# A twelve-block decoder on one core: GpSimd order, early first scores and a vector-engine causal mask in the last stage

## The reference, cut to what matters

```python
# stage 3x: linear cross attention, 16 heads of 16; f(x) = x + 1 if x > 0 else exp(x)
q = f(query @ Wq.T); gate = sigmoid(query @ Wg.T + bg); k, v = split(kv @ Wkv.T); k = f(k)
z = 1 / (q . k.sum(-2) + EPS)
out = (q @ (k^T v) * z) * gate @ Wo.T

# stage 3f: B_, S, D = 8, 128, 256; F_ = 1024; R = 16; H = 16; HD = 16
x = _rmsnorm(hidden_states, ln1_w)
scores = einsum('bqhd,bkhd->bhqk', q, k) / sqrt(HD)
scores = where(causal, scores, finfo.min)
attn = einsum('bhqk,bkhd->bqhd', softmax(scores), v) @ Wo.T
mod = 0.1 * tanh(attn @ A)
h = _rmsnorm(residual, ln2_w)
gate = silu(h @ W_in_base.T + mod * (h @ A) @ B)
up = h @ W_up_base.T
return residual + gate * up @ W_down.T
...
x = x + _L3_xattn_ref(_layernorm(x), ctx, ...)
x = x + _L3_ffn_ref(_layernorm(x), ...)
```

## Time and profile before

| | us |
|---|---|
| median of 3 runs | 2128.72 |
| lowest, highest of the 3 | 2124.98, 2131.11 |
| the profiled execution | 2125.13 |
| its span, first to last instruction | 2123.4 |

### The profile page before, as it was taken

How to read it: one execution, slowest core, us unless ns; L and a number is a source line. 1 busy time by engine, 2 the same in 40 slices (tenths; PEclk the granted TensorE clock), 3 DMA queues, 4 the chain that set the end, 5 groups by cost and what they waited for, 6 DMA issues and landing times.

```text
span 2123.4 us, 31457 instructions
## 1 busy us (share of the span) xinstructions
PE 1850.7 (87%) x11530; PEld 1378.9 (65%) x11530; DVE 1470.8 (69%) x2483; ACT 1073.9 (51%) x2328; POOL 1088.7 (51%) x797
## 2 busy tenths in 40 slices
PE   7577779789899987899999999868888789998999
PEld 6111148545689965677777777757777565566887
DVE  5698952456764476777777776589999978855453
ACT  4444421334322254666666666566666656654443
POOL 2599950211692065655555554599999840022321
PEclk9688989689899999999999999989999999999999
DMA  4211001130400000110000001000000020000000
GB/s 161 48 35 35 0 1 40 38 159 0 179 1 1 1 21 21 50 34 1 1 2 1 1 1 40 20 1 1 1 1 1 25 76 7 1 1 1 6 9 8
DMA packets 22177, 54.88 MB, mean 26 GB/s; under 512 B 8591, under 2 KB 13752, under 8 KB 19592
## 3 DMA queue, kind: packets, MB, share of 16 engines
q1 hardware_dynamic: 22024, 52.88, 7.4%
HBM read 44.48 MB, written 1.05 MB: 21 GB/s over the span
## 4 chain that ended last, share of the span: by engine, by line
PE 54%; DVE 18%; POOL 11%; issue 9%; ACT 7%; SPq 1%; DMA 0%; DVEq 0%; POOLq 0%; ACTq 0%
POOL sbuf L1310 4%; PE psum L4136 4%; DVE sbuf L2302 4%; PE psum L4199 3%; PE psum L3490 2%; DVE psum L3113 2%; POOL sbuf L1318 2%; PE psum L4296 2%; PE psum L4583 1%; PE psum L4604 1%; PE psum L4590 1%; PE psum L4168 1%; PE psum L4184 1%; PE psum L4140 1%; PE psum L4148 1%
## 5 line engine op out<-in xcount | busy, mean ns | idle before, releaser
L1310 POOL TENSOR_TENSOR sbuf<-sbuf 128x1035 f32<-128x1035 f32 x128 | 248.2, 1967 | 0.9 <-ACT sbuf L1952 0.9
L4296 PE MATMUL psum<-sbuf 128*128 128x128 f32 (+1 forms) x1024 | 144.8, 292 | 60.9 <-ACT sbuf L1979 45.4
L1979 ACT ACTIVATE sbuf<-sbuf 128x1001 f32<-128x1001 f32 (+1 forms) x128 | 141.8, 1138 | 101.1 <-DVE sbuf L3121 69.0
L4296 PEld LDWEIGHTS psum<-sbuf 128*128 128x128 f32 (+1 forms) x1024 | 126.3, 153 | 82.3 <-ACT sbuf L1979 63.9
L1265 POOL TENSOR_TENSOR sbuf<-sbuf 128x512 f32<-128x512 f32 x64 | 66.7, 1042 | 184.8 <-DVE sbuf L2985 184.8
L1111 POOL TENSOR_TENSOR sbuf<-sbuf 128x1024 f32<-128x1024 f32 x64 | 149.9, 2355 | 15.9 <-DVE sbuf L2302 15.1
L2302 DVE TENSOR_TENSOR_SCAN sbuf<-psum,sbuf 128x1024 f32<-128x1024 f32 x64 | 144.6, 2277 | 13.7 <-ACT psum L1439 7.0
L3438 PE MATMUL psum<-sbuf 96*128 96x512 bf16 x256 | 84.2, 440 | 74.9 <-DVE sbuf L2302 32.3
L1893 ACT ACTIVATE sbuf<-psum,sbuf 128x128 f32<-128x128 f32 x256 | 90.4, 365 | 107.2 <-DVE sbuf L2979 107.2
L1439 ACT ACTIVATE psum<-psum,sbuf 128x1016 f32<-128x1016 f32 x64 | 68.9, 1081 | 125.3 <-PE psum L3438 125.3
L3113 DVE SCALAR_TENSOR_TENSOR psum<-sbuf,psum 128x1024 f32<-128x1024 f32 (+1 forms) x96 | 122.2, 1273 | 12.3 <-PE psum L4286 5.3
(11 more groups left out here) (809 smaller groups left out, 5105.3 us busy)
## 6 DMA issues: line engine op xcount, KB each, us to landing
sbuf<-sbuf SPq DMA_DIRECT2D x42, 128.0 KB, 2.4
sbuf<-w_p_d SPq DMA_DIRECT2D x8, 512.0 KB, 3.8
sbuf<-w_qkv_d SPq DMA_DIRECT2D x3, 768.0 KB, 4.2
sbuf<-w_e_d SPq DMA_DIRECT2D x1, 2048.0 KB, 7.8
sbuf<-w_gu_d SPq DMA_DIRECT2D x1, 2048.0 KB, 9.0
sbuf<-w_gu_d SPq DMA_DIRECT2D x2, 1024.0 KB, 7.7
sbuf<-w_dn_d SPq DMA_DIRECT2D x1, 2048.0 KB, 15.8
sbuf<-w_q_d SPq DMA_DIRECT2D x1, 2048.0 KB, 8.0
```

What stands on the lines that cost most here:

```text
L1310: pool.tensor_tensor(P_r[g % 7][:, :, :], rows.unsqueeze(2).to_broadcast([128, 23, 45]), cols.unsqueeze(1).to_broadcast([128, 23, 45]), AL ...
L1979: act.activation(Q_r[g % 6][:, 0:w], Q_r[g % 6][:, 0:w], ACT.Silu, scale=q8_p[n % 2][:, h:h + 1]).then_inc(silu_done, 1)
L4296: last = pe.matmul(Gps[0:m, c, :], Q_r[g % 6][:, 128 * c:128 * c + m], ident[:, :], start=h == 0 and c % 4 == 0, stop=h == 7, skip_group_c ...
```

## The change

The diff does the following.

- POOL, stage 3x: in each turn `L3x_unit(i + 3)` is called ahead of `L3x_softplus(i + 1)`.
- The first element's steps of stage 3f move up. On PE: transposes from turn 6 to 5, q and k from 7 to 6, value and scores from behind the loop to turn 8 ahead of `L3x_project(7)`; the product `L3f_woap` goes ahead of `L3x_project(6)`. On ACT: `L3f_unT(0)` and `L3f_qTc(0)` go to the top of turns 6 and 7. On DVE: `L3f_keys(0)` goes into turn 7.
- The mask: the four matmuls of each `L3f_scores` go. `L3f_max` first adds the mask (f32, broadcast over the 8 heads) to the scores in PSUM and writes `L3f_P` in SBUF, waits for that, and takes the maximum from SBUF; `L3f_sub` works in place on `L3f_P`. The wait for the transposes of the element before moves from `L3f_sub` to `L3f_max`.
- The order in a pass of stage 3f: on ACT `L3f_qTc(i + 1)` behind both `L3f_exp`; on DVE `L3f_keys(i + 1)` behind both `L3f_sums`; on PE `L3f_ups(i - 1, 1)` ahead of `L3f_value(i + 1)`.

```diff
@@ POOL, stage 3x
             for i in range(-1, 8):
+                if i < 5:
+                    L3x_unit(i + 3)
                 if i < 7:
                     L3x_softplus(i + 1)
-                if i < 5:
-                    L3x_unit(i + 3)
                 if i >= 0:
                     L3x_logs(i)
@@ ACT, stage 3x and 3f
             for i in range(9):
+                if i == 6:
+                    L3f_unT(0)
+                if i == 7:
+                    L3f_qTc(0)
                 if i < 6:
                     L3x_kexp(i + 2)
...
-                if i == 6:
-                    L3f_unT(0)
                 if i == 7:
                     act.wait_ge(woa_done, 1)
                     act.activation(L3f_woa[:, :, :], L3f_woap[:, :, :], ACT.Copy).then_inc(woac_done, 1)
-                    L3f_qTc(0)
...
-                if i < 7:
-                    L3f_qTc(i + 1)
                 if i < 8:
                     L3f_exp(i, 0)
                     L3f_exp(i, 1)
                 if i < 7:
+                    L3f_qTc(i + 1)
                     L3f_vc(i + 1)
@@ DVE
             def L3f_max(n, a):
                 dve.wait_ge(score_done, L3f_start['score'] + n + 1)
                 if n > 0:
-                    dve.wait_ge(sub_done, L3f_start['sub'] + 2 * n + a - 1)
-                dve.tensor_reduce(L3f_mx[a][:, :], L3f_S8[a][:, :, :], AX.X, ALU.max).then_inc(max_done, 1)
+                    dve.wait_ge(pT_done, L3f_start['pT'] + 2 * n + a - 1)
+                dve.tensor_tensor(L3f_P[a][:, :, :], L3f_S8[a][:, :, :], causal[:, None, :].to_broadcast([128, 8, 128]), ALU.add).then_inc(mask_done, 1)
+                dve.wait_ge(mask_done, L3f_start['mask'] + 2 * n + a + 1)
+                dve.tensor_reduce(L3f_mx[a][:, :], L3f_P[a][:, :, :], AX.X, ALU.max).then_inc(max_done, 1)
             def L3f_sub(n, a):
                 dve.wait_ge(max_done, L3f_start['max'] + 2 * n + a + 1)
-                if n > 0:
-                    dve.wait_ge(pT_done, L3f_start['pT'] + 2 * n + a - 1)
-                dve.tensor_tensor(L3f_P[a][:, :, :], L3f_S8[a][:, :, :], L3f_mx[a][:, :].unsqueeze(2).to_broadcast([128, 8, 128]), ALU.subtract).then_inc(sub_done, 1)
+                dve.tensor_tensor(L3f_P[a][:, :, :], L3f_P[a][:, :, :], L3f_mx[a][:, :].unsqueeze(2).to_broadcast([128, 8, 128]), ALU.subtract).then_inc(sub_done, 1)
...
+                if i == 7:
+                    dve.wait_ge(const_done, L3f_start['const'] + 1)
+                    L3f_keys(0)
                 if i < 8:
                     L3x_quotient(i)
                 if i > 0:
                     L3x_resid(i - 1)
-            dve.wait_ge(const_done, L3f_start['const'] + 1)
-            L3f_keys(0)
             L3f_hidden(1)
...
-                if i < 7:
-                    L3f_keys(i + 1)
                 if i < 8:
                     L3f_sums(i, 0)
                     L3f_sums(i, 1)
+                if i < 7:
+                    L3f_keys(i + 1)
@@ PE
-                for r in range(4):
-                    pe.matmul(L3f_S[:, r, :, :, :], idb[:, :], L3f_causal[:, None, :].to_broadcast([128, 4, 128]), start=True, stop=False)
                 for c in range(2):
                     for r in range(4):
-                        last = pe.matmul(L3f_S[:, r, c, :, :], L3f_qT[32 * r:32 * r + 32, c, :], L3f_kM[32 * r:32 * r + 32, c, :, :], start=False, stop=c == 1)
+                        last = pe.matmul(L3f_S[:, r, c, :, :], L3f_qT[32 * r:32 * r + 32, c, :], L3f_kM[32 * r:32 * r + 32, c, :, :], start=True, stop=True)
...
                 if i < 8:
                     L3x_readout(i)
-                if i > 0:
-                    L3x_project(i - 1)
-                if i == 6:
-                    pe.wait_ge(L3f_w_loaded, 144)
-                    pe.wait_ge(L3x_unT_done, 8)
-                    L3f_uTr(0)
                 if i == 7:
...
                     last.then_inc(woa_done, 1)
+                if i == 8:
+                    L3f_value(0)
+                    pe.wait_ge(woac_done, 1)
+                    L3f_scores(0)
+                if i > 0:
+                    L3x_project(i - 1)
+                if i == 5:
+                    pe.wait_ge(L3x_unT_done, 8)
+                    L3f_uTr(0)
+                if i == 6:
+                    pe.wait_ge(L3f_w_loaded, 144)
                     L3f_qk(0)
-            L3f_value(0)
-            pe.wait_ge(woac_done, 1)
             for i in range(9):
-                if i < 8:
+                if 0 < i < 8:
                     L3f_scores(i)
...
                 if i > 0:
                     L3f_gates(i - 1, 1)
+                if i > 0:
+                    L3f_ups(i - 1, 1)
                 if i < 7:
                     L3f_value(i + 1)
                 if i > 0:
-                    L3f_ups(i - 1, 1)
                     L3f_adapt(i - 1, 1)
                     L3f_downs(i - 1, 0)
```

More of the change, by code:

```diff
@@ L707, in build_program @@
         L3f_start = {'const': 10, 'bn': 54, 'stats': 70, 'u': 46, 'uT': 34, 'unT': 34, 'q': 81, 'v': 84, 'ss': 68, 'lnvar': 85, 'rstd': 85, 'vc': 92,
-                     'qTc': 81, 'kTc': 84, 'score': 116, 'max': 128, 'exp': 136, 'recip': 92, 'prob': 68, 'pT': 120, 'pTc': 120, 'o': 92, 'cat': 79,
-                     'proj': 108, 'resid': 60, 'sub': 64, 'ur': 8, 'xr': 16, 'mod': 4, 'low': 4, 't': 4, 'gate': 20, 'up': 20, 'silu': 144,
-                     'prod': 136}
+                     'qTc': 81, 'kTc': 84, 'score': 116, 'mask': 129, 'max': 128, 'exp': 136, 'recip': 92, 'prob': 68, 'pT': 120, 'pTc': 120,
+                     'o': 92, 'cat': 79, 'proj': 108, 'resid': 60, 'sub': 64, 'ur': 8, 'xr': 16, 'mod': 4, 'low': 4, 't': 4, 'gate': 20, 'up': 20,
+                     'silu': 144, 'prod': 136}
         L0a_later_loaded = stack.enter_context(nc.semaphore('L0a_later_loaded'))
```

## The result

The changed kernel takes **2113.73 us** (median of 8 runs, 2110.47 to 2119.49) beside 2127.84 for the kernel before (8 runs, 2123.36 to 2136.62): a ratio of 0.9933, 95% interval 0.9915 to 0.995, or 14.1 us less. The forecast was 2120.2 and its range began at 2114. The direction and each place of the gain were right, the size was too small: 8.5 us were forecast. The profiled execution after took 2114.61 with a span of 2112.9, so the two traced executions differ by 10.5. Of the eight executions after, five lie between 2110.47 and 2114.61 and three between 2119.27 and 2119.49.

The account below looks back on a forecast made before the run. PE, busy for all of a 22.4 us pass of stage 3f, was taken as the bound. Head -6.0, passes -2.6 and tail +0.1 sum to -8.5 us: 2120.2 against the median 2128.72, range 2114 to 2127.

Parts of the forecast that it names:

- the head's 6.0: Start of stage 3f: first element's steps moved up, so the second scores end at 1947.6, 6.0 us earlier.
- So I keep that level: Head of stage 3f: value (1.76) and transposes (3.87) kept at granted clock 0.50; at full clock the gain would be 8.6.
- POOL's order: Stage 3x: unit ahead of softplus removes five PE waits at the transposes, 4.7 us in all.
- the first mask: Head of stage 3f: first mask starts at about 1928.0, where the first maximum started at 1936.66.
- taking the difference between two executions off a median: Whole kernel: the 8.5 us worked out from the profiled execution (2125.13) was subtracted from the three-run median, 2128.72.
- A first pass longer than 20 us: Stage 3f, first pass: listed as a sign that the prediction is wrong.
- The clock of the head: Head of stage 3f: clock stays at 0.50 for value and transposes; value to second scores takes 8.9 us.
- The passes: Stage 3f: mask off PE gives 0.97, keys' new place takes 0.53 back; 21.93 per pass, six give 2.6 us.
- The tail: Behind the eighth scores: ups of the second half wait for their product; plus 0.1 to 0.3 us, taken as 0.1.
- The Trainium skill's 1.38 us: Rival, ACT in stage 3f: a drain after each table change makes passes 23.3 and the total 2129.6; chance 0.01.
- The slower rival: Stage 3f: in-place subtract with both operands in SBUF takes 2.64 beside POOL, not 1.22; +9.8 us, 2138.5; chance 0.07.
- More than forecast: Rival: clock stays full in the first pass (-8.6) and keys are never late (5.8); -14.3, 2114.4; chance 0.12.

Follow-up runs that it names:

- warm: Changed kernel plus 24 spare matmuls behind q and k of the second element, in PE's first-pass wait for the keys; 2112.75 us, ratio 0.9945 to the kernel before.
- pe_mask: Changed kernel with the four mask matmuls back on PE and the old maximum and subtract; 2115.44 us, ratio 0.9963 to the kernel before.
- no_mask: Changed kernel with the causal mask left out altogether; 2114.75 us, ratio 0.9939 to the kernel before.
- early_keys: Changed kernel with the keys placed between the two sums of a pass instead of behind both; 2109.71 us, ratio 0.9917 to the kernel before.
- pool_busy: Changed kernel with four spare adds on POOL from the end of each pass's scores; 2139.28 us, ratio 1.0045 to the kernel before.
- pool_only: Kernel before with one edit, unit ahead of softplus on POOL in stage 3x; 2121.11 us, ratio 0.9988 to the kernel before.
- pool_fill: pool_only with ten spare matmuls in PE's waits of turn 7; 2118.95 us, ratio 0.9976 to the kernel before.

## Why the prediction was right in direction and too small

The step that failed in the traces is the head's 6.0: it was 7.9. Of these 1.9 us, 1.3 are the clock ("so I keep that level") and 1.0 is POOL's order, less 0.4 at the first mask. The step that failed beyond the traces is taking the difference between two executions off a median.

**POOL's order: right, mis-sized.** The waits of the 3x transposes are gone. The term was the sum of five idle times, 4.7; the last transposes came 5.7 earlier. Each of the five waits cost about 0.2 more than its idle time: a turn of 6.35 stands where 7.56 stood with an idle time of 1.00, a difference of 1.21. In the traces, where the ends of matmuls are modelled, a matmul that waits for nothing starts before the one ahead has ended (1864.37 + 1.88 = 1866.25, the next at 1866.09), and a wait takes that overlap too.

**The first mask: right.** 18.72 from the transposes to the mask, where the prediction's 1928.0 - 1909.7 is 18.3; from the mask to value 10.66 (10.7 forecast). The last transposes were 1.1 earlier than forecast and the mask 0.7. The vector engine's steps of 1.26 and 1.14 and the chain over keys held. "A first pass longer than 20 us" can't count as a sign of being wrong: the forecast's own ends of the scores, 1925.7 and 1947.6, are 21.9 apart, and the measured ones 20.6.

**The clock of the head: the step that failed most in the traces.** "So I keep that level": value did run slowly (2.08 for 1.76), but the clock came back within the transposes, which took 2.44 where 3.87 was kept from before. The prediction took over how slow the matmuls had been and not when the clock fell: with a longer idle time ahead, it fell 3.9 us before value and not behind its start, and over half of its 6.8 us low were spent waiting. From value to the second scores it was 7.62 instead of 8.9 (8.3 and 8.4 in the two traces with a second fall). The head gave 7.9 in this pair of traces (96.56 - 88.62), not 6.0; warm shows the part of the clock that was left, 1.2 to 2.0.

**The passes: right.** 21.91 against 21.93, six of them 2.73 for 2.6, with the wait at value for the keys in its place. pe_mask, no_mask and early_keys show the three terms apart: the mask matmuls 0.97, the mask adds nothing, the keys' place 0.5 to 0.6. PE's wait was 0.35 where 0.53 stood: the start of value was right to 0.01, and the 0.2 is the overlap again.

**The tail: right.** The ups waited 0.17; the tail is 0.26 longer (35.85 for 35.59), at the upper end of 0.1 to 0.3.

**The rivals.** Table loads are not followed by a drain in the trace after either: 1973.92 + 1.28 = 1975.20, the exponential at 1975.21. The Trainium skill's 1.38 us of "What ACT_TABLE_LOAD costs" ("ScalarE: Activation LUTs") would by the prediction's estimate have made passes of 23.3, and they are 21.91. The slower rival's condition, POOL busy beside the subtract, did not arise; pool_busy shows that its price was too low. "More than forecast", 2114.4, came nearest to the time, but not by its mechanism: the clock fell, and the keys were late in each pass.

**The 3.6 us beyond the traces: not explained.** The forecast took the difference between two executions off a median. The medians differ by 14.1, the two traced executions by 10.5, and more traces do not close the gap: the four traced executions of before took 2125.13, 2123.92, 2122.70 and 2124.70, the four of after 2114.61, 2114.08, 2113.70 and 2112.64, and their means are 10.4 apart. The stretch from `L3x_unit(0)` alone gives more, 268.45 before and 256.30 after, 12.2 apart, because two of the four traces of before have the fall in turn 7. The changed kernel no longer waits 1.7 at `L3x_project` there, and no trace of it, nor of the nine variants built on the new head, has that fall. But the two executions with the fall are not slower in total, so it isn't shown to be what the medians have on top. The executions without a trace spread further than the traced ones: the kernel before reaches 2136.62 and its slowest traced execution is 2125.13; the kernel after reaches 2119.49 and its slowest traced one is 2114.61. What those longer executions contain, these runs don't show. Why the clock falls behind the same wait in some executions and not in others also stays open.

## What to carry to other kernels

A wait that an engine order can remove is worth its idle time plus the overlap that it breaks (0.2 us for each PE wait here). One trace is one sample: a wait of 1.7 us on PE that was harmless in one execution cost 3.2 us up to the first scores in another, through the clock that fell behind it, so compare several traces before a wait is priced. A slow stretch of the clock is not a property of the matmuls that it hit: ask where it begins when the waits move. Work given to the vector engine is free only where the next thing in its order also waits for another engine; find the step that it delays (here the keys), and move that one as well: placing the keys between the sums gave 0.62 us in each pass.

## What the runs showed of the hardware

- A vector subtract of 128x1024 f32 with both operands in SBUF took 3.0 to 3.3 us beside POOL's adds, and 1.22 without them; it ended 1.08 behind the POOL add under way, and the next POOL add took 3.34 instead of 2.35. The mask add of the same size, with one operand in PSUM, kept 1.22 beside them.
- The granted clock fell in turn 7 in two of four traces of one and the same kernel, and where it fell, it stood at 0.50 for 6.8 us, across matmuls that follow each other without a gap.
- The stretch from `L3x_unit(0)` was 263.33 in pool_only and 261.92 with ten spare matmuls in PE's waits (pool_fill), one trace each; the ratios, 0.9988 and 0.9976, point the same way with intervals that overlap.
